# Graph network layers on one core: the products of exponents and gathered rows in the fourth pass go from VectorE to POOL

## The chip, the cores and the metric

The kernel runs on one core of one Trainium2 chip. The metric is the device time of one execution in microseconds. The kernel before took 10,931.24 us (median of 3 runs, 10,926.27 to 10,934.09).

## What is computed

A graph of 12,500 nodes with 64 features each and 212,500 edges, sorted by destination, goes through four layers. Each takes `h = max(layernorm(x), 0)` and adds its result to `x`:

```python
x = x + segment_sum((h * W)[src], dst)                      # layer 0
x = x + sage_conv(relu(sage_conv(h)))                       # layer 1: two means over neighbours
x = x + layer2(h, edge_attr)                                # layer 2: softmax over the edges of a node
x = x + segment_sum(h[src] @ W.T + b, by source) / degree   # layer 3
```

Layer 2 is the one that the change touches. With `eh = edge_attr @ W_fcr.T`, `ex = exp(eh - m[dst])` and `z = (h @ W_fc.T)[src]`:

```python
alpha = ex / segment_sum(ex, dst)
agg = segment_sum(alpha * (z + eh), dst)
```

The kernel divides at the end: for every node it sums `ex`, `ex * eh` and `ex * z` over the edges, and takes (the second + the third) / the first.

## The kernel before

Edges are cut into G = 208 groups of 1024, a group into CH = 8 columns of 128 edges, one edge in each partition. Nodes are cut into T = 98 tiles of 128. There are five passes over all groups (`p` = 0 to 4), since layer 1 needs two. In each pass:

- POOL (L270 to L286) gathers, for each group, the rows of the edges' source nodes from a table in memory, with 8 indirect DMAs of 128 rows (L283), into one of SLOTS = 8 slots of a ring (`ring`, in the fourth pass `ring3`, 64 float32 a row; in the trace both belong to the tile `flat`). So a pass has 208 x 8 = 1664 gathers. Before a group it waits for the slot to be free (`slots_free`, L279), and before each eighth group for the list of indices (`staged`).
- SyncE (L318 to L344) waits for the rows of each group to land, signals `rows_ready` (L334), loads the next index lists, and in the fourth pass, `p` = 3, also waits for the loaded exponents (`exl`, L333) and loads those of three groups ahead (`load_ex`, L309) as soon as TensorE has begun group g (`ex_free`). The exponents, `ex` and `ex * eh` for each edge, were written to memory in the second pass. They go to `exr`, which has XR = 4 buffers of 8 x 192 float32: columns 0 to 63 `ex`, 64 to 127 `ex * eh`, 128 to 191 room for `ex * z`.
- VectorE builds one-hot matrices (L418, in the fourth pass L686) that say which node of the tile an edge belongs to. In the fourth pass it also multiplies: `product(g)` (L667 to L672) waits for `rows_ready`, writes `ex * z` into columns 128 to 191 of `exr`, and signals `slots_free`, which both POOL (the slot of the ring is free) and TensorE (the group is ready) wait for. It stands in front of the two halves of the group's one-hots (L679), whose buffers are handed back by TensorE (`more_free`).
- TensorE multiplies one-hots and rows into the tile's sums in PSUM (L926, in the fourth pass L1080). A group that two tiles share is visited twice.
- After every seventh tile (14 times a pass) VectorE works on the batch of seven (L707 to L714, and the norm and split at L436 to L455), and the rows of the next pass's table are written by ScalarE's queue. The next pass's gathers wait until the last batch is written (L273).

Engines run their queues in order. POOL's and SyncE's are unrolled, VectorE's and TensorE's are loops over tiles and groups.

Of the kernel before, what the change touches and what calls it, by code (L numbers as in the profile page):

```python
# [6 lines left out]
N, F, E, HID = 12500, 64, 212500, 128  # L7
T = -(-N // P)

CH = 8  # L10
GE = CH * P
G = -(-E // GE)
SLOTS = 8
# [14 lines left out]
F1, F3 = F + 1, 3 * F  # L28
D3 = 3 * F1
TW = D3 + 1  # L30
XR = 4
# [22 lines left out]
def gnn_kernel(nc, x, first_dst, dst_blk, dst_cols, src_cols, src_keys, dst_keys, ea2, w0, w1, b1, w2, b2, wfcr, wfc,  # L54
# [3 lines left out]
    ALU = mybir.AluOpType  # L58
    ACT = mybir.ActivationFunctionType
    AX = mybir.AxisListType  # L60
    ds = bass.ds
    ctx = ExitStack()
    with ctx:
# [21 lines left out]
        ring3 = flat[:, 0:SLOTS * CH * F * 4].bitcast(fp32).rearrange("p (s k c) -> p s k c", s=SLOTS, k=CH)  # L85
# [94 lines left out]
        exl = [sem(f"exl{i}") for i in range(XR)]  # L180
# [65 lines left out]
        @block.gpsimd  # L246
        def _(pool):
            pool.memset(ident[:, :], 0.0).then_inc(s_const, 1)
            pool.memset(ones[:, :], 1.0).then_inc(s_const, 1)
            pool.memset(bits, 1.0).then_inc(s_const, 1)  # L250
            pool.memset(tw[:, :, :], 0.0).then_inc(s_const, 1)
            pool.memset(epsc[:, :], 1e-5).then_inc(s_const, 1)
            pool.memset(zb[:, :], 0.0).then_inc(s_const, 1)
            pool.memset(wbd[:, :], 0.0).then_inc(s_const, 1)
            pool.iota(iota[:, :], pattern=[[1, 4 * P]], base=0, channel_multiplier=0,
                      allow_small_or_imprecise_dtypes=True).then_inc(s_const, 1)
            pool.iota(tpos[:, :], pattern=[[P, T]], base=0, channel_multiplier=0,
                      allow_small_or_imprecise_dtypes=True).then_inc(s_const, 1)
            pool.iota(thr[:, :], pattern=[[P, T]], base=P, channel_multiplier=0,
                      allow_small_or_imprecise_dtypes=True).then_inc(s_const, 1)  # L260
            pool.wait_ge(s_const, 10)
            pool.affine_select(out=ident[:, :], in_=ident[:, :], compare_op=ALU.not_equal, fill=1.0, base=0,
                               pattern=[[-1, P]], channel_multiplier=1).then_inc(s_const, 1)

            for b in range(NK - LK):
                pool.memset(bits[:, b * P:(b + 1) * P].rearrange("p (u v w) -> p u v w", v=2, w=1 << b)[:, :, 1, :],
                            -1.0).then_inc(s_const, 1)
            pool.memset(tw[:, :, F:F1], 1.0).then_inc(s_const, 1)

            for p in range(5):  # L270
                s = q[p]
                rows_at = landed[p // 3]
                pool.wait_ge(s_tab[p], 16 if p == 0 else 16 * NBAT)  # L273
                for g in range(G):
                    slot, st = g % SLOTS, g // SG % 2
                    if g % SG == 0:
                        pool.wait_ge(staged[st], 16 * (p * (G // SG // 2) + g // SG // 2 + 1))
                    if g >= SLOTS:
                        pool.wait_ge(s["slots_free"], g - SLOTS + 1)  # L279
                    for k in range(CH):  # L280
                        c = g % SG * CH + k
                        to_row = ring3[:, slot, k, :] if p == 3 else ring[:, slot, k, 0:(TW if p in (0, 4) else F3)]
                        pool.indirect_dma_start(  # L283
                            out=to_row, out_offset=None, in_=tables[p],
                            in_offset=bass.IndirectOffsetOnAxis(ap=stage[:, st, c:c + 1].bitcast(u32), axis=0),
                        ).then_inc(rows_at[slot], 16)  # L286

        @block.sync
        def _(sp):
            sp.dma_start(xs[:, :, :], x).then_inc(s_in, 16)  # L290
            sp.dma_start(g0i[:, :], first_dst).then_inc(s_in, 16)
            sp.dma_start(w0s[:, :], w0.partition_broadcast(P)).then_inc(s_in, 16)
            sp.dma_start(b2s[:, :], b2.partition_broadcast(P)).then_inc(s_in, 16)
            sp.dma_start(b1s[:, :], b1).then_inc(s_in, 16)
            sp.dma_start(dst_i, dst_cols).then_inc(s_in, 16)
            for dst, src in ((w1s, w1), (w2s, w2), (wts, wfc), (lws, loop_w), (w3s, w3b)):
                sp.dma_start(dst[:, :], src).then_inc(s_in, 16)  # L297
            sp.dma_start(wzu[:, 0:F], wfc_t).then_inc(s_in, 16)
            sp.wait_ge(s_const, 10)
            sp.dma_start(wbd[0:F, 0:F], wfcr).then_inc(s_in, 16)  # L300
            sp.dma_start(wbd[F:P, F:P], wfcr).then_inc(s_in, 16)

            def load_stage(n, of):

                sp.dma_start(stage[:, n % 2, :], of[:, n * SG * CH:(n + 1) * SG * CH]).then_inc(staged[n % 2], 16)

            def load_ex(g):

                half, at = (0, g) if g < G2 else (1, G - 1 - g)  # L309
                sp.dma_start(exr[:, g % XR, :, 0:2 * F],  # L310
                             ex_d[half, LEAD + at * GE:LEAD + (at + 1) * GE, :].rearrange("(k p) c -> p k c", p=P)
                             ).then_inc(exl[g % XR], 16)

            sp.wait_ge(s_in, 16 * NIN)
            load_stage(0, src_cols)
            load_stage(1, src_cols)
            NL = G // SG
            for p in range(5):  # L318
                s = q[p]
                if p == 2:  # L320
                    for h in range(2):
                        sp.wait_ge(b_st[h], 32 * (STEPS // 2))
                    sp.dma_start(src_k, src_keys).then_inc(k_in, 16)
                    sp.dma_start(dst_k, dst_keys).then_inc(k_in, 16)
                if p == 3:
                    sp.wait_ge(k_idx, 1)
                    for g in range(XR - 1):
                        load_ex(g)
                for g in range(G):
                    sp.wait_ge(landed[p // 3][g % SLOTS], CH * 16 * (G // SLOTS * (p % 3) + g // SLOTS + 1))  # L330
                    if p == 3:
                        settle(sp)
                        sp.wait_ge(exl[g % XR], 16 * (g // XR + 1))  # L333
                    sp.sem_inc(s["rows_ready"], 1)  # L334
                    if g % SG == SG - 1:
                        n = g // SG + 2
                        if n < NL:
                            load_stage(n, sidx if p == 4 else src_cols)
                        elif p < 4:
                            load_stage(n - NL, sidx if p == 3 else src_cols)  # L340
                    if p == 3 and g + XR - 1 < G:
                        if g >= 1:
                            sp.wait_ge(s["ex_free"], g)
                        load_ex(g + XR - 1)  # L344
            sp.wait_ge(s_out, 16 * NBAT)

        @block.vector
        def _(dve):
# [315 lines left out]

            s3 = q[3]

            def product(g):  # L667
                dve.wait_ge(s3["rows_ready"], g + 1)
                V.tensor_tensor(exr[:, ds(g % XR, 1), :, 2 * F:F3].rearrange("p o k c -> p (o k) c"),  # L669
                                exr[:, ds(g % XR, 1), :, 0:F].rearrange("p o k c -> p (o k) c"),  # L670
                                ring3[:, ds(g % SLOTS, 1), :, :].rearrange("p o k c -> p (o k) c"),
                                ALU.mult).then_inc(s3["slots_free"], 1)  # L672

            def build_f(t, a):
                base = fixed[:, a % 4 * P:(a % 4 + 1) * P].unsqueeze(1).to_broadcast([P, CH // 2, P])

                def visit(g, v, first):
                    if not first:
                        product(g)  # L679
                    for half in range(2):  # L680
                        k = half * (CH // 2)
                        if first:
                            dve.wait_ge(s3["oh_free"], t * 2 + (half + 1))
                        else:
                            dve.wait_ge(s3["more_free"], g * 2 + (half - 1))
                        V.tensor_tensor(ohf[not first][:, k:k + CH // 2, :], base,  # L686
                                        dcol[:, ds(g * CH + k, CH // 2)].unsqueeze(2).to_broadcast([P, CH // 2, P]),
                                        ALU.is_equal).then_inc(s3["oh_ready" if first else "more_ready"], 1)
                return visit

            dve.sem_inc(s3["more_ready"], 1)
            product(0)
            with dve.Fori(0, TURNS) as i:
                ga = hots(s3, N3, i, 0, load_last(dve, 0, i * UT), 0, build_f(i * UT, 0))
                for a in range(UT):
# [485 lines left out]
```

## Time and profile before

| | |
|---|---|
| median of 3 runs | 10,931.24 us |
| profiled execution | 10,930.99 us |
| its span in the trace | 10,929.1 us |
| POOL busy | 8175.2 us, of them 8170.5 us gathers |
| VectorE busy | 3852.7 us |
| TensorE busy | 3899.8 us |
| ScalarE busy | 476.7 us |

An engine's busy time doesn't count the register, semaphore and DMA-issuing instructions. A gather counts as busy on POOL while its transfers are being described there, not until its rows have landed. The span is 1.9 us shorter than the execution's own time.

### The profile page before, as it was taken

To read this page: it belongs to the slowest core of one execution; us is meant where nothing else is said; L and a number is where in the kernel's file an instruction comes from. 1 tells how busy PE (TensorE), PEld (TensorE's weight loads), DVE (VectorE), ACT (ScalarE), POOL (GpSimd) and SP (SyncE) were. 2 spreads that over 40 slices of the span, in tenths; PEclk is the share of its full clock that TensorE was granted. 3 is DMA by queue.
4 is the path that set the end of the run, shared out by engine and by line. 5 is a ranking of instruction groups with operands and counts; after the bars stand their busy time and mean duration, and the time that the engine had idled before them with its cause. 6 is when DMAs were issued, how large, how long until landed. Compare 5 with 4: busy or idle time off the path is not lost.

```text
span 10929.1 us, 84376 instructions
## 1 busy us (share of the span) xinstructions
PE 3899.8 (36%) x18630; PEld 3008.6 (28%) x18631; DVE 3852.7 (35%) x4123; ACT 476.7 (4%) x740; POOL 8175.2 (75%) x8343
## 2 busy tenths in 40 slices
PE   1323333334444444222222224555555532222222
PEld 1212112223333333211111113554555521111111
DVE  4333333343443444354444432333333321222221
ACT  0000000011111111000000000000000000000000
POOL 4777777777777777777777777777777767777777
PEclk8666666666676666555555556777777755555555
DMA  4444344444554554312333312333333322222222
GB/s 101 112 108 114 100 105 114 108 133 149 150 155 141 160 156 137 88 39 55 62 63 62 63 39 60 81 81 77 84 81 81 81 45 42 42 42 42 42 42 40
DMA packets 712000, 950.46 MB, mean 87 GB/s; under 512 B 289345, under 2 KB 504385, under 8 KB 709453
## 3 DMA queue, kind: packets, MB, share of 16 engines
q0 software_dynamic: 266240, 385.62, 17.4%
q10 hardware_dynamic: 208528, 441.95, 13.5%
q1 hardware_dynamic: 236931, 119.79, 3.8%
q14 instruction: 224, 1.84, 0.1%
q8 instruction: 77, 1.26, 0.0%
HBM read 739.75 MB, written 206.15 MB: 87 GB/s over the span
## 4 chain that ended last, share of the span: by engine, by line
POOL 74%; issue 23%; DVE 1%; DMA 1%; PE 1%; SPq 0%; ACT 0%; DVEq 0%; ACTq 0%; POOLq 0%
POOL flat L283 74%; DMA flat<-table,stage 0%; DMA table<-flat 0%; PE pair L926 0%; SPq L297 0%; PE flip L997 0%; DMA wbd<-in_wfcr 0%; DVE flat L383 0%; DVE flat L381 0%; DVE flat L376 0%; DVE hk L375 0%; DVE flat L367 0%; DVE hk L366 0%; DVE dinv L368 0%; DVE has L364 0%
## 5 line engine op out<-in xcount | busy, mean ns | idle before, releaser
L283 POOL DMA_INDIRECT flat<-table,stage x8320 | 8170.5, 982 | 2736.8 <-issue 2532.3
L926 PE MATMUL pair<-flat 128*128 x9760 | 1610.0, 339 | 5649.3 <-SPq L334 5142.5
L926 PEld LDWEIGHTS pair<-flat 128*128 x9760 | 1173.5, 132 | 6130.5 <-issue 6067.8
L1080 PE MATMUL pair<-flat 128*128 x4880 | 1156.8, 408 | 949.2 <-DVE flat L686 949.0
L418 DVE TENSOR_TENSOR flat<-fixed,dcol 128x1024 f32 x915 | 1078.2, 1217 | 1164.5 <-PE pair L926 1032.8
L1080 PEld LDWEIGHTS pair<-flat 128*128 128x128 f32 x4880 | 1077.3, 247 | 1021.3 <-issue 1018.5
L460 DVE TENSOR_REDUCE batch<-pair 128x65 f32<-128x195 f32 (+1 forms) x392 | 140.3, 358 | 2908.9 <-PE pair L951 2908.9
L418 DVE TENSOR_TENSOR flat<-fixed,flat 128x1024 f32 x305 | 362.6, 1221 | 735.8 <-PE pair L926 680.9
L669 DVE TENSOR_TENSOR flat<-flat (+1 forms) x208 | 143.9, 692 | 1261.2 <-SPq L334 1261.2
L940 PE MATMUL wide<-flat,wbd 128*128 128x512 f32 x840 | 533.6, 787 | 135.6 <-DMA flat<-gate_d 102.1
L686 DVE TENSOR_TENSOR flat<-fixed,dcol 128x512 f32<-128x512 f32 x610 | 392.8, 683 | 40.1 <-DVE fixed L411 20.2
L997 PE MATMUL flip<-ident,flat 128*128 128x128 f32 x840 | 312.6, 381 | 75.3 <-DVE flat L533 65.6
L940 PEld LDWEIGHTS wide<-flat,wbd 128*128 128x128 f32 x840 | 210.6, 268 | 357.1 <-issue 356.3
L490 DVE TENSOR_TENSOR_SCAN flat<-flat,wide 128x1536 f32<-128x1536 bf16 x70 | 238.9, 3412 | 185.1 <-PE wide L940 183.8
L998 PE MATMUL flip<-ident,flat 128*128 128x128 f32 x840 | 294.0, 360 | 0.0
L822 ACT ACTIVATE flat<-flip 128x512 f32<-128x512 f32 x420 | 248.9, 597 | 801.8 <-PE flip L998 795.2
L779 ACT ACTIVATE sd<-var,epsc 128x7 f32<-128x7 f32 x42 | 12.6, 300 | 5477.2 <-DVE var L441 5477.2
L525 DVE TENSOR_TENSOR_SCAN flat<-flat,carry 128x1536 f32<-128x1536 bf16 x70 | 238.7, 3410 | 10.9 <-DMA flat<-gate_d 10.7
L997 PEld LDWEIGHTS flip<-ident,flat 128*128 128x128 f32 x840 | 183.4, 218 | 129.1 <-issue 121.6
L578 DVE TENSOR_TENSOR flat<-flat 128x1024 f32<-128x1024 f32 x171 | 209.4, 1224 | 5.3
L579 DVE TENSOR_TENSOR flat<-flat 128x1024 f32<-128x1024 f32 x171 | 208.7, 1220 | 0.0
L998 PEld LDWEIGHTS flip<-ident,flat 128*128 128x128 f32 x840 | 190.3, 227 | 0.0
(142 smaller groups left out, 1809.8 us busy)
## 6 DMA issues: line engine op xcount, KB each, us to landing
flat<-table,stage POOLq DMA_INDIRECT x8320
flat<-in_ea ACTq DMA_DIRECT2D x140, 768.0 KB, 6.4
ex_d<-flat ACTq DMA_DIRECT2D x140, 768.0 KB, 5.2
flat<-ex_d SPq DMA_DIRECT2D x208, 512.0 KB
flat<-gate_d ACTq DMA_DIRECT2D x280, 192.0 KB, 7.3
pm_d<-flat ACTq DMA_DIRECT2D x70, 768.0 KB, 4.3
flat<-pm_d ACTq DMA_DIRECT2D x70, 768.0 KB
sort_d<-flat ACTq DMA_DIRECT2D x14, 1024.0 KB, 4.0
```

The lines of the kernel that those rows point to most:

```text
L283: pool.indirect_dma_start(out=to_row, out_offset=None, in_=tables[p], in_offset=bass.IndirectOffsetOnAxis(ap=stage[:, st, c:c + 1].bitcast ...
L418: V.tensor_tensor(ohb[:, ds(v % OHB, 1), :, :].rearrange("p o k e -> p (o k) e"), base, col[:, ds(g * CH, CH)].unsqueeze(2).to_broadcast([ ...
L490: V.tensor_tensor_scan(pm[h], gate[h], eh, pm[1 - h][:, SB - 1:SB], ALU.add, ALU.max).then_inc(f_scan, 1)
L525: V.tensor_tensor_scan(mx[:, ::-1], gate[h][:, ::-1], pm[h][:, ::-1], carry[:, :], ALU.add, ALU.max).then_inc(b_scan, 1)
L578: kstep(V.tensor_tensor(y0, x0, x1, ALU.min))
L686: V.tensor_tensor(ohf[not first][:, k:k + CH // 2, :], base, dcol[:, ds(g * CH + k, CH // 2)].unsqueeze(2).to_broadcast([P, CH // 2, P]), ...
L822: S.activation(exo[h][:, :, 4 * j:4 * j + 4, :], flip[(u0 + j) % 2].rearrange("p (m a c) -> p a m c", m=4, a=2), ACT.Copy).then_inc(s1["fl ...
L926: mm = M(bank[a % 2][:, 0:width], flat[:, ds(at_one[k], P * 2)].bitcast(bf16), flat[:, ds(at_row[k], TW * 2)].bitcast(bf16)[:, 0:width], s ...
L940: mm = M(wide[:, c * 512:(c + 1) * 512], wbd[:, :], ea[h][:, c * 512:(c + 1) * 512], start=True, stop=True)
L997: TP(flip[u % 2][:, n * 2 * P:n * 2 * P + P], pm[h][:, cols], ident[:, :])
L998: mm = TP(flip[u % 2][:, n * 2 * P + P:(n + 1) * 2 * P], xe[:, cols], ident[:, :])
L1080: mm = M(bank[a % 2][:, 0:F3], ohf[not first][:, k, :], exr[:, ds(g % XR, 1), k, :].rearrange("p o c -> p (o c)"), start=first and k == 0, ...
```

## The change

In the fourth pass POOL does the multiplication itself. In its loop, before the gathers of group g, it multiplies for group g − 2; the last two groups' products follow after the last gathers. It waits by itself for the group's rows (`landed`) and exponents (`exl`). SyncE no longer waits for the exponents nor signals `rows_ready` in this pass, and VectorE's `product` is gone from the loop.

```diff
+            def product(g):
+
+                pool.wait_ge(landed[1][g % SLOTS], CH * 16 * (g // SLOTS + 1))
+                pool.wait_ge(exl[g % XR], 16 * (g // XR + 1))
+                nc.gpsimd.tensor_tensor(exr[:, g % XR, :, 2 * F:F3], exr[:, g % XR, :, 0:F], ring3[:, g % SLOTS, :, :],
+                                        ALU.mult).then_inc(q[3]["slots_free"], 1)
+
             for p in range(5):
                 s = q[p]
                 rows_at = landed[p // 3]
                 pool.wait_ge(s_tab[p], 16 if p == 0 else 16 * NBAT)
                 for g in range(G):
+                    if p == 3 and g >= 2:
+                        product(g - 2)
                     slot, st = g % SLOTS, g // SG % 2
...
                         ).then_inc(rows_at[slot], 16)
+                if p == 3:
+                    product(G - 2)
+                    product(G - 1)
...
                     if p == 3:
                         settle(sp)
-                        sp.wait_ge(exl[g % XR], 16 * (g // XR + 1))
-                    sp.sem_inc(s["rows_ready"], 1)
+                    else:
+                        sp.sem_inc(s["rows_ready"], 1)
...
-            def product(g):
-                dve.wait_ge(s3["rows_ready"], g + 1)
-                V.tensor_tensor(exr[:, ds(g % XR, 1), :, 2 * F:F3].rearrange("p o k c -> p (o k) c"),
-                                exr[:, ds(g % XR, 1), :, 0:F].rearrange("p o k c -> p (o k) c"),
-                                ring3[:, ds(g % SLOTS, 1), :, :].rearrange("p o k c -> p (o k) c"),
-                                ALU.mult).then_inc(s3["slots_free"], 1)
-
...
                 def visit(g, v, first):
-                    if not first:
-                        product(g)
                     for half in range(2):
...
             dve.sem_inc(s3["more_ready"], 1)
-            product(0)
```

## Rows read from the trace of the kernel before

**Rows 1.** The page's first part: busy us, share of the span, instructions.

```profile
PE 3899.8 (36%) x18630; PEld 3008.6 (28%) x18631; DVE 3852.7 (35%) x4123; ACT 476.7 (4%) x740; POOL 8175.2 (75%) x8343
```

**Rows 2.** The chain that ended last: shares of the span by engine.

```profile
POOL 74%; issue 23%; DVE 1%; DMA 1%; PE 1%; SPq 0%; ACT 0%; DVEq 0%; ACTq 0%; POOLq 0%
```

**Rows 3.** Fourth and fifth pass: stretch, length, busy us of each engine.

```profile
6709.00:8836.00 2127.00, 1158.93 (x4982) 1086.30 (x4982) 728.70 (x1172) 5.02 (x16) 1594.22 (x1661) 0.74 0.33 80
8836.00:10920.00 2084.00, 530.36 (x2816) 389.54 (x2817) 434.76 (x484) 21.11 (x39) 1569.94 (x1664) 0.51 0.21 42
```

**Rows 4.** VectorE's two largest groups, 6709 to 8836: busy, mean ns | idle before.

```profile
L686 DVE TENSOR_TENSOR flat<-fixed,dcol 128x512 f32<-128x512 f32 x610 | 392.8, 683 | 40.1 <-DVE fixed L411 20.2 <-issue 17.2
L669 DVE TENSOR_TENSOR flat<-flat x207 | 143.2, 692 | 1253.0 <-SPq L334 1253.0
```

**Rows 5.** Waits, 6709 to 8836: us in total, times, longest.

```profile
PE pair L1080 <- DVE flat L686: 949.0, 201, 21.5
```

**Rows 6.** Timeline, fourth pass: start us, us, engine line operation [idle before].

```profile
7302.13 0.94 POOL L283 DMA_INDIRECT flat<-table,stage  x1 [0.30 <-issue]
7302.63 0.69 DVE L669 TENSOR_TENSOR flat<-flat  x1 [6.62 <-SPq L334]
...
7303.37 0.94 POOL L283 DMA_INDIRECT flat<-table,stage  x1 [0.30 <-issue]
```

**Rows 7.** Timeline, beside a batch of tiles in the fourth pass.

```profile
7325.81 0.63 DVE L714 SCALAR_TENSOR_TENSOR xs<-batch,xs 128x448 f32 x1 [0.22 <-DVE batch L712]
7325.92 1.33 POOL L283 DMA_INDIRECT flat<-table,stage  x1 [0.30 <-issue]
...
7327.56 1.23 POOL L283 DMA_INDIRECT flat<-table,stage  x1 [0.30 <-issue]
```

**Rows 8.** Timeline, the sort in the third pass.

```profile
5238.26 1.22 DVE L579 TENSOR_TENSOR flat<-flat 128x1024 f32<-128x1024 f32 x1
5238.31 1.99 POOL L283 DMA_INDIRECT flat<-table,stage  x1 [0.30 <-issue]
```

**Rows 9.** POOL's groups with shapes, whole span: busy us, mean ns | idle before.

```profile
L250 POOL MEMSET cat<- 128x896 f32 x1 | 0.8, 841 | 0.0
...
L255 POOL IOTA iota<- 128x512 f32 x1 | 0.6, 552 | 0.0
L262 POOL TENSOR_SCALAR_AFFINE_SELECT ident<-ident 128x128 f32<-128x128 f32 x1 | 0.3, 293 | 0.2 <-POOL thr L259 0.2
...
L248 POOL MEMSET ident<- 128x128 f32 x1 | 0.2, 204 | 0.3 <-POOLq L1172 0.3
```

**Rows 10.** POOL's timeline: two memsets, and the first gathers of all.

```profile
0.92 0.84 POOL L250 MEMSET cat<- 128x896 f32 x1
1.70 1.24 POOL L251 MEMSET tw<- 128x1372 bf16 x1
...
124.09 1.10 POOL L283 DMA_INDIRECT flat<-table,stage  x1 [118.70 <-DMA table<-flat]
```

**Rows 11.** Timeline, the end of the fourth pass and the start of the fifth.

```profile
8802.78 4.80 PE L1080 MATMUL pair<-flat 128*128 x16 [5.30 <-DVE flat L686]
...
8807.50 2.79 PE L1080 MATMUL pair<-flat 128*128 x16
8808.24 0.94 POOL L283 DMA_INDIRECT flat<-table,stage  x1 [0.30 <-issue]
...
8811.15 0.69 DVE L669 TENSOR_TENSOR flat<-flat  x1 [6.51 <-SPq L334]
...
8812.64 4.54 PE L1080 MATMUL pair<-flat 128*128 x16 [2.35 <-DVE flat L686]
...
8836.04 0.94 POOL L283 DMA_INDIRECT flat<-table,stage  x1 [26.85 <-DMA table<-tw]
```

## The prediction

> **What bounds the kernel now.** I read the page's busy shares first. POOL is busy 75% of the span, VectorE 35%, TensorE 36%: only one engine comes near the end time [rows 1]. The chain that ended last says the same more sharply: 74% of the span is the one POOL line L283, the gathers, and 23% is "issue", the time in which that engine waited for nothing that the profile shows [rows 2]. Together 97%. So the question is what stands in POOL's queue, and everything else is cover until proven otherwise.
>
> Then the same by pass. The fourth pass lies between 6709 and 8836 us and takes 2127 us; the fifth, which has no product, takes 2084 us [rows 3]. In the fourth pass the gathers take 1594 us of POOL and their "issue" gaps most of the rest. VectorE has about 1400 us free there [rows 3], and spends 1253 us of it in front of the product, waiting for the rows to land [rows 4]. TensorE waits 949 us for VectorE's one-hots in the whole pass [rows 5]. Both are waiting for POOL in turn. Nothing that VectorE gives up here can by itself shorten the pass.
>
> The timeline of one group shows the mechanism. A gather takes 0.94 us, and the next starts 0.30 us after its end: 1.25 us from start to start, 10 us for the eight of a group [rows 6]. The reader should look at what happens when a gather is stretched: one of 1.33 us is followed by the same gap of 0.30 us, so that the start-to-start time grows to 1.64 us [rows 7]. The gap isn't slack that soaks up a longer predecessor. POOL works off its queue strictly in turn, and whatever is added to it is added to the time, unless it is different in kind from a stretched gather.
>
> **The change, part by part.**
>
> *Removed from VectorE:* 208 products of 0.69 us, 143 us [rows 4]. They lie in the 1253 us in which VectorE waits anyway. Worth nothing on the path by themselves. Could they be worth something by freeing the gathers? Some VectorE instructions do stretch gathers: in the sort of the third pass a gather that starts while a multiply-like instruction with two SBUF inputs runs takes 1.99 instead of 0.94 us [rows 8]. The product is of that kind. But in the fourth pass it runs from 0.5 us after one gather's start until 0.05 us before the next one's, and both neighbours take 0.94 us [rows 6]. The bound on the gain is the difference of the gathers' busy time between the fourth and the fifth pass, 1594 − 1570 = 24 us [rows 3]; most of it must belong to the batch work between tiles, beside which the stretched gathers stand [rows 7]. I take 5 us for the products' part.
>
> *Added to POOL:* 208 products of 128x512 float32 elements with two SBUF inputs. The trace has no such instruction on POOL, so I bound it. A memset of 896 columns takes 841 ns and one of 128 columns 204 ns: 0.83 ns a column for a stream that is written, and about 0.10 us fixed; the iota of 512 columns, also only written, takes 552 ns, as that line gives [rows 9]. The affine select, which reads one stream and writes one, takes 293 ns for 128 columns, 89 ns more than the memset: 0.70 ns a column for a stream that is read. A product writes one and reads two: 0.10 + 512 x 0.83 ns + 2 x 512 x 0.70 ns = 1.24 us. Low end: the second input costs nothing, 0.88 us. High end: 1.24 us, and a second gap of 0.30 us because the product stands between two gathers, and 0.16 us, by which the first gather after arithmetic was longer than the others [rows 10]: 1.70 us. For the gap I take none beyond the one that the following gather has anyway, since POOL's memsets follow each other with no gap (start at 0.92, 0.84 us long, next start at 1.70) [rows 10]. 208 x 1.24 = 258 us; the ends are 208 x 0.88 = 183 and 208 x 1.70 = 354 us.
>
> The Trainium skill prices this instruction directly: "GPSIMD Engine Reference", section "Elementwise — side-by-side cycle accounting", gives 4497 ns for a GpSimd add of two float32 operands of 2048 columns against 2293 ns on VectorE, about 2.6 cycles an element. A quarter of it is an estimate of 1.12 us, and with that the added time would be 234 us and the total 11,171 us. No row of this case shows it; VectorE's own product here takes 0.69 us.
>
> *The new waits on POOL.* Each product waits for the rows of the group two back and for that group's loaded exponents. The last of these gathers was issued a whole group, 10 us, earlier, and the old product shows how long a landing takes: it started 1.97 us after the end of the last gather (8809.18 to 8811.15), the hop over SyncE included [rows 11]. So the row wait is met. The exponents are loaded three groups ahead. What is queued behind a wait here is every later gather, so a missed one would show at full price. A wait that is met costs nothing that I can see: the gathers at the group's edges, where the kernel before waits too, have the gap of 0.30 us as all others. The old wait for a free slot is now met by POOL itself.
>
> *SyncE* no longer waits for the exponents or signals; its loads come up to two groups later, because TensorE starts a group later. The load for group g+3 goes out when TensorE has begun group g, now some 1.5 us into the gathers of g+2; the product of g+3 stands three groups of gathers later, over 30 us. Cost nothing. TensorE takes 4.8 us for a visit [rows 11], and a group will last 11.2 us; it keeps its cover.
>
> *Next to the batch work* POOL's product can meet VectorE instructions with two SBUF inputs, each 0.63 us, and wait for one of them, as the gathers do [rows 7, 8]. 14 batches, one product each: up to 14 x 0.63 = 9 us. I take 5 us. It cancels the 5 us above.
>
> *The end of the pass.* The fifth pass can't start until the last batch has its table written. Before, the last gather ended at T = 8809.18 us and TensorE's last visit at 8817.18, T + 8.0; the fifth pass began at 8836.04 [rows 11]. Now the last two products come after the last gather. That of the last but one is done at T + 0.30 + 1.24 = T + 1.5; its visits take 4.8 and 2.8 us (it is shared by two tiles), to T + 9.1; the last group's visit takes 4.5 us more, to T + 13.7. 5.7 us later than before, all on the path.
>
> Sum, against the profiled execution of 10,931 us (span 10,929.1 and 1.9 us around it; the median of the runs is 10,931.2, the same): 10,931 + 258 − 5 + 5 + 6 = **11,195 us**, 2.4% slower.
>
> **The rivals.**
>
> *A, near the forecast but dear:* POOL pays each change between gather and arithmetic, with the second gap and the longer first gather: 354 instead of 258 us, 11,291 us. For it: the 1.10 us of the first gather [rows 10]. Against: that is one gather after a long wait, and the memsets show no gap. 17%.
>
> *B, cheap:* the second input is nearly free, 0.88 us a product, 11,120 us. For it: POOL reads and writes at once, and an affine select does more per element than a multiplication. Against: two inputs need two reads. 15%.
>
> *C, not slower at all:* the product vanishes in the gaps. Eight gathers leave 8 x 0.30 = 2.4 us a group in which POOL computes nothing; if this is time in which the queue hands over the next gather while the cores idle, a product of 1.24 us can run in it, and since 1.24 is under 2.4 the pass keeps its length: 10,931 − 5 + 6 = 10,932 us. It decides in this way as long as the product is shorter than the gaps it can reach, and the gap shrinks behind a longer predecessor. Against: behind the stretched gathers it doesn't shrink by a hundredth [rows 7]. 4%.
>
> *D, a reload or a serial wait:* POOL's product has to wait for more than its own work, for the gathers' writes to drain or for a transfer. The gathers drain in the 1.97 us of the landing [rows 11], so 208 x (1.97 + 1.24) = 668 us, 11,600 us. Against: the waits named are for the group two back. 4%.
>
> **How the numbers follow.** 60% for the forecast with its own spread of some 30 us for the product's price, 17% for A, 15% for B, 4% for C, 4% for D. The range takes in A and B with the rounding of their other terms, 11,105 to 11,300 us, and leaves out C, D and a little beside A. A measurement of this kernel tells a difference from none at about 0.2%, 22 us. Slower by over that: all but C, 0.96. C comes out within it, 0.03 of its 0.04; 0.01 is left for C with the gathers gaining all of the 24 us, which would be faster.
>
> **What would show it.** Right: 208 products on POOL in the fourth pass, about 1.24 us each; the gathers still 0.94 us with gaps of 0.30 us; a group of 11.2 us; no idle time on POOL in front of a product beyond a gap's length; VectorE with no wait for SyncE in the pass, and TensorE waiting for POOL instead; the fourth pass about 2390 us and the others as before; the way from the last gather to the fifth pass some 6 us longer. A gap of 0.30 us on both sides of a product speaks for A, under 0.9 us for B, a pass of unchanged length for C, a long idle time before the products for D. Wrong would be above all the price of an instruction that the trace doesn't show: 0.1 us there is 21 us in the end.

## The result and the profile after

The changed kernel takes 11,172.11 us (median of 4 runs, 11,164.82 to 11,177.93) against 10,930.5 us: ratio 1.0219, 95% interval 1.0206 to 1.0232. It is 242 us slower; 264 us were predicted. The profiled execution has a span of 11,174.7 us.

The page's first part and the chain of work that ended last, of the kernel after, in the form of [rows 1] and [rows 2]:

```profile
PE 3965.5 (35%) x18630; PEld 3071.5 (27%) x18631; DVE 3762.7 (34%) x3915; ACT 477.6 (4%) x740; POOL 8449.7 (76%) x8551
...
POOL 75%; issue 23%; DVE 1%; DMA 1%; PE 0%; SPq 0%; ACT 0%; POOLq 0%; DVEq 0%; ACTq 0%
```

POOL, which was the bound, has 208 instructions and 275 us more (265 us of them are the products), and VectorE, which had time to spare, 90 us less. By pass (start and end in us, length, busy us of the engines) the fourth and the fifth, to be held against [rows 3]:

```profile
6711.00:9079.00 2368.00, 1228.62 (x5002) 1154.19 (x5002) 640.37 (x964) 9.21 (x22) 1859.62 (x1872) 0.72 0.29 72
9079.00:11165.00 2086.00, 526.50 (x2813) 388.88 (x2814) 434.25 (x483) 21.12 (x39) 1571.83 (x1664) 0.52 0.21 42
```

From its first gather to the first of the fifth pass, the fourth took 2131.3 us before (6704.70 to 8836.04) and takes 2368.4 us now (6710.91 to 9079.31): 237 of the 246 us by which the span grew. Six more lie ahead of the pass, in code that is the same in both; in the experiments below on unchanged code the fourth pass began anywhere from 6691 to 6713 us, so these six say nothing.

What a group looks like now, POOL's part of the timeline (start us, us, engine, line, operation, idle before), against [rows 6]:

```profile
7303.38 0.94 POOL L292 DMA_INDIRECT flat<-table,stage  x1 [0.30 <-issue]
7304.34 1.27 POOL L274 TENSOR_TENSOR flat<-flat 128x512 f32<-128x512 f32 x1
7305.77 0.98 POOL L292 DMA_INDIRECT flat<-table,stage  x1 [0.16 <-POOL flat L274]
7307.06 0.95 POOL L292 DMA_INDIRECT flat<-table,stage  x1 [0.30 <-issue]
...
7314.56 0.94 POOL L292 DMA_INDIRECT flat<-table,stage  x1 [0.30 <-issue]
7315.53 1.27 POOL L274 TENSOR_TENSOR flat<-flat 128x512 f32<-128x512 f32 x1
```

Read the gaps, not only the durations. The product starts 0.02 us behind the gather, and behind the product the next gather starts after 0.16 us instead of 0.30. So 0.12 us of the usual gap are gone, and 0.03 to 0.04 us come back in a gather of 0.98 us. So a product of 1.27 us costs 1.27 − 0.09 = 1.18 us, and 206 of them (the last two stand behind the last gather) 243 us. The median group agrees: 11.18 us, against 9.99 before.

Who waits for whom in the pass (us in total, times, longest), against [rows 4, 5]:

```profile
DVE flat L689 <- PE pair L1082: 1530.2, 372, 24.1
...
PE pair L1082 <- POOL flat L274: 927.3, 182, 16.4
```

VectorE no longer waits for SyncE and builds its one-hots ahead; TensorE now waits for POOL's product. Neither gets the pass any further, because both follow POOL.

The end of the pass, against [rows 11]:

```profile
9048.41 1.27 POOL L274 TENSOR_TENSOR flat<-flat 128x512 f32<-128x512 f32 x1
9049.98 5.27 PE L1082 MATMUL pair<-flat 128*128 x16 [5.69 <-POOL flat L274]
9050.00 1.27 POOL L274 TENSOR_TENSOR flat<-flat 128x512 f32<-128x512 f32 x1 [0.32 <-DMA flat<-table,stage]
...
9055.16 5.39 PE L1082 MATMUL pair<-flat 128*128 x32
...
9079.31 0.98 POOL L292 DMA_INDIRECT flat<-table,stage  x1 [28.04 <-DMA table<-tw]
```

From the last gather's end (9048.38) to the fifth pass it is 30.9 us instead of 26.9: 4.1 us more.

### The profile page after: what moved, and what is told of

Read it like the earlier page. It is cut to its first block, busy times and chain, and to the rows that moved or that the text cites. A ratio compares the mean times of both kernels' runs of the same rounds, so it can differ in the third digit from the quotient of the medians.

```text
span 11174.7 us, 83548 instructions
## 1 busy us (share of the span) xinstructions
PE 3965.5 (35%) x18630; PEld 3071.5 (27%) x18631; DVE 3762.7 (34%) x3915; ACT 477.6 (4%) x740; POOL 8449.7 (76%) x8551
## 4 chain that ended last, share of the span: by engine, by line
POOL 75%; issue 23%; DVE 1%; DMA 1%; PE 0%; SPq 0%; ACT 0%; POOLq 0%; DVEq 0%; ACTq 0%
POOL flat L292 73%; POOL flat L274 2%; DMA table<-flat 0%; PE pair L1082 0%; DMA flat<-table,stage 0%; SPq L309 0%; DMA flat<-ex_d 0%; DVE hk L387 0%; DVE flat L393 0%; DVE flat L388 0%; DVE hk L378 0%; DVE flat L395 0%; DVE flat L379 0%; DVE has L376 0%; DVE dinv L380 0%
## 5 line engine op out<-in xcount | busy, mean ns | idle before, releaser
L928 PE MATMUL pair<-flat 128*128 x9760 | 1609.0, 339 | 5664.7 <-SPq L346 5178.4
L1082 PE MATMUL pair<-flat 128*128 x4880 | 1222.1, 425 | 1120.4 <-POOL flat L274 927.3
L1082 PEld LDWEIGHTS pair<-flat 128*128 128x128 f32 x4880 | 1142.0, 260 | 1193.9 <-issue 1189.9
L274 POOL TENSOR_TENSOR flat<-flat 128x512 f32<-128x512 f32 x208 | 264.9, 1274 | 3.9 <-DMA flat<-table,stage 0.3
```

Of the source, the lines that this page charges most:

```text
L274: nc.gpsimd.tensor_tensor(exr[:, g % XR, :, 2 * F:F3], exr[:, g % XR, :, 0:F], ring3[:, g % SLOTS, :, :], ALU.mult).then_inc(q[3]["slots_f ...
L928: mm = M(bank[a % 2][:, 0:width], flat[:, ds(at_one[k], P * 2)].bitcast(bf16), flat[:, ds(at_row[k], TW * 2)].bitcast(bf16)[:, 0:width], s ...
L1082: mm = M(bank[a % 2][:, 0:F3], ohf[not first][:, k, :], exr[:, ds(g % XR, 1), k, :].rearrange("p o c -> p (o c)"), start=first and k == 0, ...
```

## Experiments

The open questions were why a product costs less than it lasts, what its price is made of (the prediction had put it together from streams that the trace showed one at a time), whether the gap can take in a short product, what VectorE's product had cost the gathers, and whether the lag of two groups is needed. All edits are to the changed kernel, but for dve_eighth. They ran in three sessions.

**The first session had stalls of its own.** In it (pool_eighth, pool_half, pool_twice, pool_slices) the kernel before took 12,820 us (median of 7) instead of 10,925. The next session, on the same chip, gave 10,924.5 us, so it wasn't the chip as such. The expectations below call this "slow transfers", but the traces don't show that. The gathers' packets took 14.9% of the span of 12,861 us in pool_eighth, 1916 us a DMA engine, against 1902 us in the kernel before and 1911 us in the changed one, and the last of a gather's 32 packets ended 1.2 us after the gather in both sessions. And TensorE, which in eighth_again (the same kernel in a later session) waited 5122 us for gathered rows outside the fourth pass, hardly waited for them now. In the first pass it was 3.8 groups behind the rows that had landed (median over its visits; eighth_again: 0.3). It stood idle with nothing in the profile to wait for. First two waits of eighth_again, then the same two of pool_eighth (us in total, times, and for most the longest):

```profile
PE pair L928 <- SPq L346: 5122.5, 682, 30.2
...
PE pair L928 <- issue: 108.9, 214, 12.0
```

```profile
  SPq L346: 35.6, 4
```

```profile
PE pair L928 <- issue: 2392.7, 628, 44.7
```

In some stretches TensorE ran one matmul at a time, with some 2 us between them, and VectorE and POOL waited:

```profile
999.00 0.94 POOL L292 DMA_INDIRECT flat<-table,stage  x1 [0.30 <-issue]
1000.07 0.32 PE L928 MATMUL pair<-flat 128*128 x1 [1.79 <-issue]
...
1002.86 0.32 PE L928 MATMUL pair<-flat 128*128 x1 [2.47 <-issue]
...
1008.26 0.94 POOL L292 DMA_INDIRECT flat<-table,stage  x1 [4.57 <-remote]
```

("remote" means that the profile shows no event that ended the wait.) What made TensorE and VectorE stall isn't known. POOL's own durations and gaps were the same to 0.01 us. Group times of these four runs are therefore medians, which leave the stalls out, and three of its four kernels were run again, under the names that end in again.

**pool_eighth and pool_half: a shorter product.** 64 and 256 of the 512 columns.

```diff
-nc.gpsimd.tensor_tensor(exr[:, g % XR, :, 2 * F:F3], exr[:, g % XR, :, 0:F], ring3[:, g % SLOTS, :, :],
+nc.gpsimd.tensor_tensor(exr[:, g % XR, 0:1, 2 * F:F3], exr[:, g % XR, 0:1, 0:F], ring3[:, g % SLOTS, 0:1, :],
```

> The changed kernel with POOL's product cut to the first 64 of 512 columns; the other seven eighths of the products are left out. Theory 1 (POOL's queue is serial; a product of n columns takes 0.10 us and 2.3 ns a column, and costs that less 0.09 us, the part of the gap it takes over): the product takes 0.25 us, a group 10.15 us, the whole 10,930 + 208 x 0.16 + 4 = 10,967 us. Theory 2 (the gap of 0.30 us between gathers is idle time that a short product can use): 0.25 is under 0.30, a group stays at 9.99 us, the whole at 10,932 us. Theory 3 (the price is mostly a fixed one of changing between gather and arithmetic): the product still takes about 1 us, the whole is above 11,100 us.

> The changed kernel with POOL's product cut to 256 of 512 columns; the other half of the products is left out. Theory 1 (0.10 us and 2.3 ns a column): the product takes 0.69 us, a group 10.59 us, the whole 10,930 + 208 x 0.60 + 4 = 11,059 us. Theory 3 (mostly a fixed price): about 11,150 us.

Measured in the first session: 12,862.7 and 12,839.4 us (one run each), and a median group of 10.23 and 10.63 us.

> The product cut to 64 columns on POOL; seven eighths are left out. The median group was 10.23 us on the chip with slow transfers. If a product adds its duration of 0.33 us less 0.09 us: 10,930 + 208 x 0.24 + 3 = 10,983 us. If the mean of that other run (13.0 us a group) is the kernel's own and not the chip's: over 11,500 us.

> The product cut to 256 columns on POOL; half is left out. 0.736 us a product, 0.64 us more a group: 10,930 + 208 x 0.64 + 3 = 11,066 us where POOL is the bound.

Measured: 10,991.9 and 11,058.9 us (one run each; kernel before: 10,921.2), a median group of 10.24 and 10.63 us. The fourth pass grew by 48 and 132 us over its 2131.3 us before. For eighth_again the total grew by 71 us where 53 were expected; the 22 us beyond the pass lie in code that is the same, in a single run. The timeline of eighth_again and of half_again:

```profile
7301.99 0.34 POOL L274 TENSOR_TENSOR flat<-flat 128x64 f32<-128x64 f32 x1
7302.49 0.98 POOL L292 DMA_INDIRECT flat<-table,stage  x1 [0.16 <-POOL flat L274]
```

```profile
7309.47 0.73 POOL L274 TENSOR_TENSOR flat<-flat 128x256 f32<-128x256 f32 x1
7310.36 0.98 POOL L292 DMA_INDIRECT flat<-table,stage  x1 [0.16 <-POOL flat L274]
```

0.33 to 0.34, 0.73 and 1.27 us for 64, 256 and 512 columns lie on a line of 0.20 us and 2.1 ns a column. The gap behind the product is 0.16 us at each length. What is added to the group, 0.25, 0.64 and 1.19 us, is each time the duration less 0.08 to 0.09 us. So a product of 0.34 us isn't hidden in a gap of 0.30 us (theory 2 falls), and the price isn't one of changing over (theory 3 falls). Theory 1 holds with another fixed part than it was given: 0.20, not 0.10 us. The Trainium skill's "GPSIMD Engine Reference", "Elementwise — side-by-side cycle accounting", has 4497 ns for 2048 columns of an addition; the line, continued to four times the longest product measured here, gives an estimate of 0.20 + 2048 x 2.1 ns = 4.5 us, the same. The prediction's quarter of it, 1.12 us, was too low since the fixed part doesn't shrink with the columns. That the total worked out from it, 11,171 us, came within 1 us of the measured one is luck: a price 0.15 us too low stood against the 0.09 us of the gap and the other terms that were off.

**pool_twice: the product made twice.**

```diff
+pool.wait_ge(s_spare, g)
+nc.gpsimd.tensor_tensor(cat[:, 0:4, :].rearrange("p b (h c) -> p (b h) c", c=F),
+                        exr[:, g % XR, :, 0:F], ring3[:, g % SLOTS, :, :], ALU.mult).then_inc(s_spare, 1)
 nc.gpsimd.tensor_tensor(exr[:, g % XR, :, 2 * F:F3], exr[:, g % XR, :, 0:F], ring3[:, g % SLOTS, :, :],
```

> The changed kernel with each product made twice on POOL, the first time into a buffer that nobody reads. Theory 1: the second stands directly behind the first and costs its full 1.27 us, since no gap of a gather is left to take over: 12.45 us a group, 11,172 + 208 x 1.27 = 11,436 us. If two products in a row overlap as the memsets at the kernel's start do, 0.05 us less each: 11,426 us. If the price lay in the change between gather and arithmetic (theory 3), the second would be nearly free: under 11,250 us.

Measured: 12,729.8 us (one run, first session), so the total says nothing on the expectation; the median group is 12.40 us, 1.22 us over that of the changed kernel.

```profile
8308.46 1.27 POOL L275 TENSOR_TENSOR cat<-flat 128x512 f32<-128x512 f32 x1
8309.68 1.27 POOL L277 TENSOR_TENSOR flat<-flat 128x512 f32<-128x512 f32 x1
8311.11 0.98 POOL L295 DMA_INDIRECT flat<-table,stage  x1 [0.16 <-POOL flat L277]
```

The second starts 1.22 us after the first, 0.05 us before its end, as POOL's memsets do [rows 10]. It costs 1.22 of its 1.27 us: again no price for the change between gather and arithmetic.

**pool_slices: eight slices between the eight gathers.**

```diff
+if p == 3 and g >= 2:
+    product(g - 2, (k,))
 c = g % SG * CH + k
```

> The changed kernel with each product cut into eight slices of 64 columns, one in front of each gather of the group. Theory 1: eight times 0.25 - 0.09 = 0.16 us, 1.28 us a group against the 1.18 us of the whole product: 11,190 us, 0.2% over the changed kernel. Theory 2 (each gap takes in a short product): eight slices of 0.25 us vanish in eight gaps of 0.30 us, 10,935 us, no slower than before. Theory 3 (a fixed price for each change): above 12,000 us.

> Eight slices of 64 columns, one in front of each gather. The traces gave 0.333 us for a slice and 11.94 us for the median group, 0.76 us more than the changed kernel's 11.18: where POOL is the bound, 11,172 + 208 x 0.76 = 11,330 us, 3.7% over the kernel before. If the gain over the kernel before that it showed where the transfers were slow belongs to the slices as such: faster than the kernel before here too, under 10,900 us.

Measured: in the first session 12,633.3 us, ratio to the kernel before 0.984 (0.981 to 0.987); in a later one 11,312.1 us, ratio 1.036 (1.034 to 1.037). The median group is 11.94 and 11.91 us, 1.9 us over the kernel before: eight times 0.33 − 0.09 = 0.24 us. The fixed part of 0.20 us is paid eight times. That is theory 1 with the measured duration; with the 0.25 us that it had been given it had come to 11,190 us. The ratio below 1 belongs to the session, not to the slices.

**pool_copy: one input instead of two.**

```diff
-nc.gpsimd.tensor_tensor(exr[:, g % XR, :, 2 * F:F3], exr[:, g % XR, :, 0:F], ring3[:, g % SLOTS, :, :],
-                        ALU.mult).then_inc(q[3]["slots_free"], 1)
+nc.gpsimd.tensor_copy(exr[:, g % XR, :, 2 * F:F3], ring3[:, g % SLOTS, :, :]
+                      ).then_inc(q[3]["slots_free"], 1)
```

> The changed kernel with a plain copy of the gathered rows on POOL in place of the product: one SBUF input instead of two, the same 512 columns; the multiplication is left out. By the streams that the prediction priced (0.10 us, 0.83 ns a column written, 0.70 ns a column read): 0.88 us, 1.27 - 0.88 = 0.39 us less a group, 11,172 - 208 x 0.39 = 11,091 us. If the second input is what costs and one input runs as fast as a memset: about 0.55 us, 11,022 us. If the number of inputs doesn't matter: 1.27 us, 11,172 us.

Measured: 11,032.4 us (one run; kernel before 10,924.5), median group 10.50 us.

```profile
7303.05 0.61 POOL L274 COPY flat<-flat 128x512 f32<-128x512 f32 x1
7303.83 0.97 POOL L292 DMA_INDIRECT flat<-table,stage  x1 [0.17 <-POOL flat L274]
```

0.62 us in the median, near the iota of 0.55 us that only writes [rows 9]: the first input is all but free, and the second (with the multiplication; the two weren't separated) costs 0.65 us. The second case of the expectation holds, and the prediction's price for each stream doesn't.

**dve_eighth: what VectorE's product had cost the gathers.** The kernel before, its product cut to 64 columns.

```diff
-V.tensor_tensor(exr[:, ds(g % XR, 1), :, 2 * F:F3].rearrange("p o k c -> p (o k) c"),
+V.tensor_tensor(exr[:, ds(g % XR, 1), 0:1, 2 * F:F3].rearrange("p o k c -> p (o k) c"),
```

> The kernel before with VectorE's product cut to 64 of 512 columns; the other seven eighths are left out. It shows what VectorE's product costs POOL's gathers. If only gathers that start while it runs are held up (16 of them in the trace of before, 5.5 us in all), nearly all of that goes and the fourth pass gets some 5 us shorter, with no gather stretched beside the product: 10,926 us. If the product costs the gathers nothing: the pass keeps its 2131 us. If it costs them the whole difference to the fifth pass: 24 us less.

Measured: 10,908.1 us (one run; kernel before 10,924.5). The gathers of the fourth pass alone (stretch, length, busy us, count), first in the kernel before, then in dve_eighth, then in the changed kernel:

```profile
6704.00:8836.00 2132.00, 1597.60 (x1664) 0.74 0.32 80
```

```profile
6691.00:8812.00 2121.00, 1588.30 (x1664) 0.74 0.32 80
```

```profile
6710.00:9079.00 2369.00, 1594.80 (x1664) 0.72 0.29 72
```

The gathers get 9.3 us shorter, and the pass, from first gather to first gather, goes from 2131.3 to 2121.5 us. About 5.5 of the 9.3 us are the 16 gathers that the timeline of before shows beginning while the product ran; the rest comes from the batch work, which meets the gathers at other moments, and so is chance rather than a price of the product. In the changed kernel a gain of that size is there too, but 206 gathers behind a product are longer by 0.03 to 0.04 us, 7 us in all. The removal was worth 9 us, not the 5 that were predicted nor 24.

**pool_lag1: the product for the group one back, ahead of the next gathers.**

```diff
-if p == 3 and g >= 2:
-    product(g - 2)
+if p == 3 and g >= 1:
+    product(g - 1)
```

> The changed kernel with POOL's product for the group one back, in front of the next group's gathers, so that it has to wait for rows that were asked for just before. Theory 1 with the landing time of the trace (1.9 us from the last gather's end): each group gets 1.6 to 1.9 us longer by the wait, less the gap it covers: 208 x 1.6 = 333 us over the changed kernel, 11,505 us. If the wait for the last rows is hidden by the gap and by what is queued: 11,172 us. The end of the pass should get about 4 us shorter, since only one product is left behind the last gather.

Measured: 11,489.7 us, ratio 1.052 (1.050 to 1.053). POOL's waits in the pass:

```profile
POOL flat L274 <- DMA flat<-table,stage: 340.1, 208, 4.4
```

1.6 us a product, and the median group goes from 11.18 to 12.68 us. The lag of two groups is needed for a product in that place: this is the wait that rival D named, for which it had put 1.97 us. In the changed kernel the same wait is 0.3 us in the whole pass.

**pool_mid: the product for the group one back, behind the fourth gather.**

```diff
+if p == 3 and g >= 1 and k == CH // 2:
+    product(g - 1)
 c = g % SG * CH + k
```

> The changed kernel with POOL's product for the group one back, in the middle of the next group's gathers (after the fourth), five microseconds after the last row was asked for. The product's price should be unchanged, 1.18 us a group. The end of the pass: only the last group's product and visit are left behind the last gather, so the way from the last gather's end to the fifth pass goes from 30.9 us to about 27.5 us: 11,168 us in all. If what costs is the product's place beside the landing or the index list rather than the product: a group of another length than 11.18 us.

Measured: 11,156.7 us, ratio 1.021 (1.020 to 1.023). The median group is 11.17 us: the product's price doesn't hang on its place. The end of the pass is shorter than expected:

```profile
9035.26 0.94 POOL L292 DMA_INDIRECT flat<-table,stage  x1 [0.30 <-issue]
...
9037.75 1.26 POOL L274 TENSOR_TENSOR flat<-flat 128x512 f32<-128x512 f32 x1 [1.54 <-DMA flat<-table,stage]
...
9039.31 2.86 PE L1081 MATMUL pair<-flat 128*128 x16 [0.29 <-POOL flat L274]
...
9060.73 0.98 POOL L292 DMA_INDIRECT flat<-table,stage  x1 [21.72 <-DMA table<-tw]
```

24.5 us from the last gather's end to the fifth pass, against 30.9 in the changed kernel and 26.9 before. Part of it is TensorE's last visit of 16 matmuls, which takes 2.9 us. One-hots that lie ready don't explain it: in pool_lag1 they lie ready too, and its last visit takes 4.8 us. The granted clock does. The last visit (in the changed kernel the last two, 32 matmuls) in the kernel before, the changed kernel, pool_mid and pool_lag1 (stretch, length, busy us of the engines, and third from the end the granted clock, 1.00 being 2.4 GHz and 0.5 the lower level of 1.2):

```profile
8812.64:8817.18 4.54, 4.54 (x17) 4.23 (x17) 0.66 (x2) 0.00 (x0) 0.00 (x0) 0.62 0.00 0
```

```profile
9055.16:9060.55 5.39, 5.39 (x35) 5.17 (x33) 0.95 (x2) 0.00 (x0) 0.00 (x0) 1.00 0.00 0
```

```profile
9039.31:9042.17 2.86, 2.86 (x17) 2.63 (x17) 0.00 (x0) 0.00 (x0) 0.00 (x0) 1.00 0.00 0
```

```profile
9375.92:9380.74 4.82, 4.82 (x17) 4.59 (x17) 0.00 (x0) 0.00 (x0) 0.00 (x0) 0.58 0.00 0
```

TensorE had been idle for 2.35 us in front of the first of these and 5.67 us in front of the last; in the changed kernel it had just ended another visit, and in pool_mid it had stood for 0.29 us. Six microseconds are below what the totals can tell apart; the trace shows them.

**changed_again.**

> The changed kernel itself once more, beside the kernel before. On a chip on which the kernel before takes about 10,930 us: 11,172 us, 2.2% slower, 11.18 us a group. Should the chip be one on which it takes about 12,820 us, as in the runs of pool_eighth, pool_half, pool_twice and pool_slices, where even the dearer slices were 1.6% faster than the kernel before: theory 1 (the transfers are the bound there and POOL's products lie in waits) expects 12,650 to 12,850 us, no slower than the kernel before; theory 2 (only the slices gain, by spreading) expects 2% slower, 13,100 us.

Measured: 11,166.6 us against 10,921.2, ratio 1.022 (1.020 to 1.024), a group of 11.19 us. Its second case, the changed kernel in a session like the first, didn't arise and stays untried.

No complete version was found that beats the kernel before in the later sessions.

## Why the prediction was right

11,195 us were predicted, 11,172 measured. Step by step:

- *The bound.* POOL's queue, strictly in turn: right. In the later sessions the fourth pass grew by 48, 105, 132 and 237 us with POOL instructions of 0.33, 0.62, 0.73 and 1.27 us (eighth_again, pool_copy, half_again, the changed kernel), which is 208 times the duration less 0.09 us, within 9 us. Nothing that VectorE was relieved of came back in time beyond 9 us.
- *The product's price:* 1.24 us predicted, 1.27 measured. The sum was right and its parts were wrong, so that it fitted is luck. The fixed part is 0.20 us, not 0.10; the first input costs almost nothing and the second 0.65 us, where 0.36 us had been taken for each and 0.42 us for the output. The affine select, the only row with an input, gave a difference of 89 ns that was taken for a price by the column; it may be mostly a fixed one, which no run separated. The errors cancelled; for one input the same sum gives 0.88 instead of 0.62 us.
- *The gap:* none beyond the usual one predicted; in fact 0.12 us of the usual one vanish and a gather gets 0.03 to 0.04 us longer, 0.09 us less a group. This is the term that was mis-sized most, 19 us in the sum: 258 predicted, 243 measured. The argument from [rows 7], that the gap is 0.30 us behind a long gather too, holds for a gather behind a gather; it didn't bear on a gap with another instruction in it. Rival C's mechanism was thus there to a small part, 0.12 us at each of the lengths that were tried. Of rival A's terms, the second gap didn't come and the longer gather was 0.03 to 0.04 us instead of 0.16.
- *The gathers relieved of VectorE's product:* 5 us predicted, 9.3 measured, of them 5.5 at the gathers that had met the product.
- *POOL's product beside the batch work:* 5 us of waiting predicted, none found. No product of the 208 took over 1.30 us. It was VectorE that waited (below).
- *The end of the pass:* 5.7 us predicted, 4.1 measured. The last visit ended at T + 12.2 us, not T + 13.7: for its length the 4.5 us of the trace of before had been taken, which were measured at a granted clock of 0.62, and it ran at 1.00 in about 2.7 us.
- *The waits on rows and exponents:* free, as argued, with 0.3 us in the pass; pool_lag1 shows that the argument was needed. It doesn't hold for a session like the first.

The sum of what was measured: 243 for the products, 9 less for the gathers, 4 for the end, 238 us against the 237 of the trace; the lengthened gathers are in the 1.18 us of a group.

## What to carry to other kernels

When one engine's queue is the whole chain, a move onto it costs nearly the moved instruction's full time on that engine (here 1.18 of 1.27 us), whatever it frees elsewhere; ask first what the other engine was waiting for. Build the price of an instruction that the trace doesn't show from a fixed part and one part for each input, and expect rows of other kinds to get the parts wrong even where the sum fits: measure it at two sizes. Before a session in which everything takes longer is put down to one cause, look at what each engine waited for: here the wait for rows had all but gone. Put an instruction that needs a landed transfer far enough behind the request (here half a group of gathers, 5 us, was enough, and none at all cost 1.6 us a time).

## What the hardware showed that wasn't expected

**POOL's product holds up VectorE.** The line of a batch's first multiplication took 0.62 us in every batch before (14 times, 624 to 626 ns) and has a median of 1.94 us after. The changed kernel's timeline:

```profile
6909.72 1.95 DVE L712 TENSOR_TENSOR batch<-batch 128x448 f32<-128x448 f32 x1
6909.91 1.27 POOL L274 TENSOR_TENSOR flat<-flat 128x512 f32<-128x512 f32 x1
6911.33 1.19 POOL L292 DMA_INDIRECT flat<-table,stage  x1 [0.16 <-POOL flat L274]
```

By its start VectorE had begun first, and yet it ended 0.49 us after POOL's product, which kept its 1.27 us. In 11 of the 14 batches this multiplication meets a product, and each time it ends 0.49 us after the product, whether its start stands 0.76 us behind the product's or 0.57 us ahead of it; the three that meet none take 0.62 us. The Trainium skill's "SBUF — State Buffer", "Who interferes with whom", says that a VectorE instruction with two SBUF inputs contends with a GpSimd instruction that reads SBUF. The trace agrees, with 1.3 us for VectorE in these lines. Where one input lies in PSUM, as that of the one-hots does, nothing is held up: 34 one-hots ran beside a product and none took over 0.69 us. The page also says that whoever issues first gets the port and that the issue order decides who blocks. The starts in the profile can't test that: a multiplication that stands 0.57 us ahead should be 0.05 us from its end when the product begins, and it ended 0.49 us after the product like the others. With VectorE busy for 640 of the pass's 2368 us, it cost nothing.

**Stalls elsewhere reach POOL, and the more so the less work it has.** In the first session the fourth pass of pool_eighth took 2743 us, against 2180 in eighth_again, and that of pool_slices, which has more POOL work, 2526 us, against 2519 in slices_again. pool_half took 2706 us against 2264, and pool_twice's 2623 us are the changed kernel's 2368 and 208 times 1.22 us. The other passes were longer in all four runs, the first 2398 to 2408 us instead of 2105 to 2111. POOL's waits in the fourth pass of pool_eighth:

```profile
POOL flat L274 <- DMA flat<-ex_d: 558.5, 59, 35.0
```

The products waited 558 us for the loaded exponents; in pool_twice the same wait is 0.2 us. In the stall shown here the load wasn't slow, it was asked for late: SyncE asks when TensorE has begun a group, and TensorE and VectorE had both been idle for 17 to 19 us. The load was asked for at 7735.39, and the product began 3.95 us later:

```profile
7734.78 0.69 DVE L689 TENSOR_TENSOR flat<-fixed,dcol 128x512 f32<-128x512 f32 x1 [18.91 <-remote]
7735.39 0.36 SPq L322 DMA_DIRECT2D flat<-ex_d  x1
...
7735.62 2.92 PE L1082 MATMUL pair<-flat 128*128 x8 [16.62 <-DVE flat L689]
...
7739.34 0.32 POOL L274 TENSOR_TENSOR flat<-flat 128x64 f32<-128x64 f32 x1 [11.34 <-DMA flat<-ex_d]
```

With more POOL work in a group the other engines have more time to catch up, which fits the numbers but was tested by no run of its own: on the mean a group took 12.0 us with the slices and 13.0 with the eighth. By this reading the kernel before, with the least POOL work, had the most to lose in that session, as the slices' ratio of 0.984 has it; there is no trace of the kernel before from it. Why the stalls came isn't settled.
